# The last batch of an adapted layer and its routed update: two half batches made one whole one

## What is computed

```python
def _L0_cond_ref(x, adapter_mapping, W, b, lora_As, lora_Bs):
    base_out = jnp.einsum('bti,oi->bto', x, W) + b
    lora_h = jnp.einsum('bti,bir->btr', x, lora_As[adapter_mapping])
    lora_out = jnp.einsum('btr,bro->bto', lora_h, lora_Bs[adapter_mapping])
    return base_out + lora_out * SCALING

def _L0_ffn_ref(x, route_w, A, Bw):
    logits = jnp.einsum('bsd,ed->bse', x, route_w)
    topk_v, topk_idx = jax.lax.top_k(logits, 1)
    route_weight = jax.nn.one_hot(topk_idx[..., 0], E, dtype=logits.dtype) * topk_v
    h = jnp.einsum('bsd,erd->bser', x, A)
    out = jnp.einsum('bser,eor->bso', route_weight[..., None] * h, Bw) * SCALING
    return out

x = x + _L0_ffn_ref(_L0_cond_ref(x, ...), route_w, A, Bw)
```

## Time and profile before

| | us |
|---|---|
| median of 3 runs (lowest, highest) | 286.09 (285.75, 286.72) |
| the profiled execution | 285.52 |
| its span, first to last instruction | 283.7 |
| PE busy | 278.7 |
| VectorE busy | 201.8 |
| ACT busy | 112.5 |
| TensorE clock granted | 1.00 throughout |

### The profile page before, as it was taken

How to read it: one execution, slowest core, us unless ns; L and a number is a source line. 1 busy time by engine, 2 the same in 40 slices (tenths; PEclk the granted TensorE clock), 3 DMA queues, 4 the chain that set the end, 5 groups by cost and what they waited for, 6 DMA issues and landing times.

```text
span 283.7 us, 4398 instructions
## 1 busy us (share of the span) xinstructions
PE 278.7 (98%) x1699; PEld 225.3 (79%) x1699; DVE 201.8 (71%) x234; ACT 112.5 (40%) x166; POOL 15.0 (5%) x46
## 2 busy tenths in 40 slices
PE   8999999999999999999999999999999999999994
PEld 5999999997766885888588758857885887588994
DVE  0052200077598999699789969996998798699975
ACT  0001301196786532734274355427432742442300
POOL 7600030000000000000000000000000000000000
PEclk9999999999999999999999999999999999999999
DMA  7999999999991066849967993999399769636668
GB/s 241 404 407 395 399 413 412 373 398 417 418 419 70 39 259 234 358 151 405 400 231 258 425 386 136 373 393 395 137 379 409 267 211 398 281 148 249 267 237 285
DMA packets 19303, 88.52 MB, mean 312 GB/s; under 512 B 2378, under 2 KB 4818, under 8 KB 11474
## 3 DMA queue, kind: packets, MB, share of 16 engines
q1 hardware_dynamic: 16128, 85.15, 76.8%
q10 hardware_dynamic: 3154, 3.09, 3.3%
HBM read 54.60 MB, written 33.55 MB: 311 GB/s over the span
## 4 chain that ended last, share of the span: by engine, by line
PE 98%; DVE 0%; DVEq 0%; issue 0%
PE bank_out L693 16%; PE bank_h L770 11%; PE bank_h L771 10%; PE bank_h L772 10%; PE bank_out L730 10%; PE bank_out L732 10%; PE bank_out L731 10%; PE bank_e L755 10%; PE bank_e L693 1%; PE bank_l L706 1%; PE bank_l L693 1%; PE bank_h L693 1%; PE bank_r L693 1%; PE bank_h L699 1%; PE bank_r L790 1%; PE bank_h L783 1%
## 5 line engine op out<-in xcount | busy, mean ns | idle before, releaser
L433 ACT ACTIVATE x_hi<-x_ring 128x1024 fp32r<-128x1024 f32 (+1 forms) x72 | 68.9, 965 | 63.5 <-PE bank_h L772 63.0
L535 DVE TENSOR_TENSOR x_lo<-x_ring,x_hi 128x1024 fp32r<-128x1024 f32 (+1 forms) x72 | 78.8, 1103 | 9.3 <-ACT x_hi L433 8.7
L628 DVE TENSOR_TENSOR x_ring<-bank_out,x_ring 128x1024 f32<-128x1024 f32 (+1 forms) x71 | 78.5, 1107 | 1.7 <-PE bank_out L732 1.3
L770 PE MATMUL bank_h<-x_hi,m_hi 128*128 128x512 f32 (+1 forms) x144 | 53.5, 372 | 0.0
L771 PE MATMUL bank_h<-x_lo,m_hi 128*128 128x512 f32 (+1 forms) x144 | 52.7, 366 | 0.0
L772 PE MATMUL bank_h<-x_hi,m_lo 128*128 128x512 f32 (+1 forms) x144 | 52.6, 366 | 0.0
L730 PE MATMUL bank_out<-wh_hi,bw_hi 128*128 128x512 f32 (+1 forms) x143 | 52.5, 367 | 0.0
L731 PE MATMUL bank_out<-wh_lo,bw_hi 128*128 128x512 f32 (+1 forms) x143 | 52.4, 366 | 0.0
L732 PE MATMUL bank_out<-wh_hi,bw_lo 128*128 128x512 f32 (+1 forms) x143 | 52.4, 366 | 0.0
L770 PEld LDWEIGHTS bank_h<-x_hi,m_hi 128*128 128x128 f32 x144 | 27.1, 188 | 11.2 <-issue 5.9
L693 PE MATMUL bank_out<-pt,w_ring 128*128 128x136 f32 x288 | 34.5, 279 | 0.0
(11 more groups left out here) (96 smaller groups left out, 188.7 us busy)
## 6 DMA issues: line engine op xcount, KB each, us to landing
x_ring<-xT SPq DMA_DIRECT2D x32, 1024.0 KB, 7.8
outT<-x_ring SPq DMA_DIRECT2D x28, 1024.0 KB, 5.0
w_ring<-W SPq DMA_DIRECT2D x30, 512.0 KB, 10.8
outT<-x_ring SPq DMA_DIRECT2D x12, 256.0 KB, 2.7
x_ring<-loraB ACTq DMA_DIRECT2D x8, 128.0 KB, 10.2
la<-loraA ACTq DMA_DIRECT2D x8, 128.0 KB, 13.1
x_ring<-BwT SPq DMA_DIRECT2D x1, 1024.0 KB, 11.6
pt<-PT SPq DMA_DIRECT2D x3, 272.0 KB, 8.9
```

Source lines behind the costliest of these rows:

```text
L433: act.activation(out, in_, ACT.Copy).then_inc(done, 1)
L535: dve.tensor_tensor(out, a, b, ALU.subtract).then_inc(done, 1)
L628: dve.tensor_tensor(x, out_banks(u, j), x, ALU.add).then_inc(v_out, 1)
L770: mm(h, m_hi[:, c, :], hi, start=(c == 0), stop=False)
```

## The change

Batch 7 is one unit of 512 tokens, like the others. The four single banks are made two tensors of two banks, `bank_eh` and `bank_rl`, of which the old names are views. The output steps of batch 7 go in turn through `bank_eh`, `bank_out0`, `bank_out1`, `bank_rl`; three output steps of batch 6 are held. Batch 7's steps are stored by 512 KB each, its last one as two chunks of 256 KB. The order of x in memory is then the same for all batches.

```diff
-        bank_e = psum("bank_e", [P, T])
-        bank_h = psum("bank_h", [P, T])
-        bank_r = psum("bank_r", [P, T])
-        bank_l = psum("bank_l", [P, T])
+        bank_eh = psum("bank_eh", [P, 2, T])
+        bank_rl = psum("bank_rl", [P, 2, T])
+        bank_e, bank_h = bank_eh[:, 0, :], bank_eh[:, 1, :]
+        bank_r, bank_l = bank_rl[:, 0, :], bank_rl[:, 1, :]
...
-        UNITS = [(b, 0, T) for b in range(NB - 1)] + [(NB - 1, t, T // 2) for t in (0, T // 2)]
-        NU = len(UNITS)
-
-        HELD = [2] * (NU - 1) + [3]
+        HELD = [2] * (NB - 1) + [3]
...
+        def w_bank(blk):
+
+            return (*bank_out, bank_eh, bank_rl)[blk] if blk < OPEN else bank_out[blk % 2]
+
+        def out_bank(b, j):
+
+            if b < NB - 1:
+                return bank_out[j % 2]
+            return (bank_eh, *bank_out, bank_rl)[j % 4]
+
+        def store_last(eng, c0, c1):
+
+            j = c0 // 2
+            k = NPIECES - NQ + 2 * T * j // PIECE
+            at = T * c0 % PIECE
+            eng.wait_ge(v_out, NP2 * (NB - 1) + (j + 1 if c1 - c0 == 2 else c1 - j))
+            eng.dma_start(outT[k, :, at:at + (c1 - c0) * T], x_ring[:, k % XRING, at:at + (c1 - c0) * T]).then_inc(d_last, 16)
...
-            for u in range(NB - 1, NU):
-                for j in range(NP2):
-                    if u < NU - 1 or j % 2 == 0:
-                        store_pair(sp, u, j)
-            store_single(sp, 1)
+            for j in range(0, NP2 - 1, 2):
+                store_last(sp, 2 * j, 2 * j + 2)
+            store_last(sp, C - 1, C)
...
             for j in range(1, NP2 - 1, 2):
-                store_pair(act, NU - 1, j)
-            store_single(act, 0)
+                store_last(act, 2 * j, 2 * j + 2)
+            store_last(act, C - 2, C - 1)
...
-            def out_pair(u, j):
-                nt = UNITS[u][2]
-                if u == 0 and j < 2:
-                    pe.wait_ge(v_m, M_LOTS[-1])
+            def out_pair(b, j):
+                if b == 0 and j < 2:
+                    pe.wait_ge(v_m, NWB)
+                elif b < NB - 1:
+                    pe.wait_ge(v_out, NP2 * b + j - 1)
+                elif j == 0:
+                    pe.wait_ge(v_two, NB)
+                    pe.wait_ge(v_wh, NB)
+                elif j == 3:
+                    pe.wait_ge(v_w, NB)
+                    pe.wait_ge(v_ahead, NB)
                 else:
-                    pe.wait_ge(v_out, pairs_added(u, j))
+                    pe.wait_ge(v_out, NP2 * b + j - (2 if j < 3 else 3))
```

More of the change, by code:

```diff
@@ L215, in loads_in_slot, with x_pair @@
             return n // WRING + (1 if n % WRING else 0)
[L217 to L223, removed]
         def x_landed(eng, k):
             eng.wait_ge(d_x[k % XRING], 16 * (k // XRING + 1))
[L229 to L234, removed]
-            nt = UNITS[u][2]
[L237 to L251, removed]
+        def x_pair(b, j):
+            at = 2 * T * j % PIECE
+            return x_ring[:, (NQ * b + 2 * T * j // PIECE) % XRING, at:at + 2 * T].rearrange("p (c t) -> p c t", c=2)
         WARM_UP = 8
@@ L437, in m_block, with split_hi @@
                 act.wait_ge(t_w, DONE[n])
[L438 to L447, removed]
+                sums = w_bank(n)[:, :, 0:PN]
+                copy(m_hi[:, 2 * n:2 * n + 2, :], sums[:, :, E:PN], a_m)
+                for i in range(2):
+                    copy(ext[i][:, 2 * n:2 * n + 2, 0:E], sums[:, :, 0:E], a_m)
+            def split_hi(b, j):
+                g = NP2 * b + j
+                if b == 0 and j < SRING:
                     act.wait_ge(t_w, NWP - WRING + j + 1)
@@ L491, in _ @@
                 m_block(n)
[L493 to L499, removed]
+            for b in range(NB):
+                act.wait_ge(t_ext, b + 1)
+                if b >= 1:
+                    act.wait_ge(v_two, b)
+                act.activation(e_top[:, :], bank_e[2 * GROUP:4 * GROUP, :], ACT.Identity,
+                               bias=e_bias[:, 0:1]).then_inc(a_top, 1)
                 for j in range(NP2):
-                    if j < 2 and short(u):
-                        split_hi(u, SRING + j)
-                    if j == 0 and leads(u):
+                    if j == 0:
                         act.wait_ge(v_two, b + 1)
@@ L507, in _ @@
                         copy(e_odd[:, :], e_two[GROUP:2 * GROUP, :], a_odd)
[L508 removed]
+                    if j == EHI_AT:
                         act.wait_ge(v_sum, b + 1)
@@ L537, in m_block, with split_lo @@
             def m_block(n):
[L538 to L546, removed]
+                dve.wait_ge(a_m, 3 * (n + 1))
+                sub(m_lo[:, 2 * n:2 * n + 2, :], w_bank(n)[:, :, E:PN], m_hi[:, 2 * n:2 * n + 2, :], v_m)
+            def split_lo(b, j):
+                g = NP2 * b + j
+                if b == 0 and j < SRING:
                     dve.wait_ge(t_w, NWP - SRING + j + 1)
@@ L610, in weight, with weigh @@
                                          op0=ALU.is_ge, op1=ALU.mult).then_inc(v_w, 1)
-            def weigh(u):
-                b, t0, nt = UNITS[u]
-                dve.wait_ge(t_main, NP2 * (u + 1))
+            def weigh(b):
+                dve.wait_ge(t_main, NP2 * (b + 1))
                 dve.wait_ge(v_w, b + 1)
[L616 to L628, removed]
+                dve.tensor_tensor(wh[:, :], bank_h, wh[:, :], ALU.mult).then_inc(v_wh, 1)
+            def weigh_lo(b):
+                dve.wait_ge(a_wh, b + 1)
+                if b >= 2:
+                    dve.wait_ge(t_out, NP2 * (b - 1))
+                sub(wh_lo[b % 2][:, :], wh[:, :], wh_hi[b % 2][:, :], v_whlo)
@@ L630, in _, with add_x @@
+            def add_x(b, j):
+                x = x_pair(b, j)
+                dve.wait_ge(t_out, NP2 * b + j + 1)
+                dve.tensor_tensor(x, out_bank(b, j)[:, :, :], x, ALU.add).then_inc(v_out, 1)
             dve.wait_ge(g_const, CONSTS)
             split_lo(0, SRING - 1)
-            for u, (b, _, _) in enumerate(UNITS):
+            for b in range(NB):
                 for j in range(NP2):
-                    if j == 0 and leads(u):
+                    if j == 0:
                         sum_two(b)
-                    if j < 2 and short(u):
-                        split_lo(u, SRING + j)
-                    if j == 0 and leads(u):
@@ L648, in _ @@
                     if j < SRING:
-                        if j >= 2 or not short(u):
-                            split_lo(u, SRING + j)
-                    elif u + 1 < NU:
-                        split_lo(u + 1, j - SRING)
-                    if u >= 1 and 1 <= j <= NP2 - HELD[u]:
-                        add_x(u - 1, j - 1)
-                if u >= 1:
-                    weigh(u)
-                    add_x(u - 1, NP2 - HELD[u])
-                weigh_lo(u)
-                if u >= 1:
-                    for j in range(NP2 - HELD[u] + 1, NP2):
-                        add_x(u - 1, j)
+                        split_lo(b, SRING + j)
+                    elif b + 1 < NB:
+                        split_lo(b + 1, j - SRING)
@@ L662, in _ @@
+                    if b >= 1 and 1 <= j <= NP2 - HELD[b]:
+                        add_x(b - 1, j - 1)
+                if b >= 1:
+                    weigh(b)
+                    add_x(b - 1, NP2 - HELD[b])
+                weigh_lo(b)
+                if b >= 1:
+                    for j in range(NP2 - HELD[b] + 1, NP2):
+                        add_x(b - 1, j)
             for j in range(NP2 - 1):
-                add_x(NU - 1, j)
+                add_x(NB - 1, j)
             for i in range(2):
-                x = x_pair(NU - 1, NP2 - 1)[:, i, :]
@@ L789, in _ @@
                             pe.wait_ge(v_w, b)
[L790 to L793 removed]
+                        mm(bank_r, beats[:, :], ahead[:, :], start=True, stop=True).then_inc(t_count, 1)
+                if b >= 1:
+                    for j in range(NP2 - HELD[b], NP2):
+                        out_pair(b - 1, j)
             for j in range(NP2):
[L795 removed]
+                out_pair(NB - 1, j)
 def kernel(x, itok_B_0_23, L0_cond_W, L0_cond_b, L0_cond_lora_As, L0_cond_lora_Bs, L0_ffn_route_w, L0_ffn_A, L0_ffn_Bw):
```

171 lines of the change are left out of this document (60 added, 111 removed).

## The result

| | before | after |
|---|---|---|
| median of 7 runs each, us | 286.09 (285.49 to 286.77) | 287.46 (287.11 to 288.00) |
| profiled execution, us | 285.52 | 287.79 |
| its span, us | 283.7 | 286.0 |
| PE matmuls | 1699 | 1602 |
| DMA engines full until about | 282.0 | 283.3 |

The account below looks back on a forecast made before the run. The stores, about 0.9 us behind the adds, were taken to bound the end. PE -1.48, wait +0.15 and VectorE's tail +0.4 were overridden by the store queue: net +0.3 on 285.52, 285.8, plus 0.57 to the median: 286.4 us, range 285.3 to 287.6.

Parts of the forecast that it names:

- PE: Batch 7's matmuls at 512 columns instead of 256: last matmul ends 1.48 us earlier, before a new wait of 0.15.
- The wait before the third held step: Batch 6's third held step must wait for VectorE's add of the first: about 0.15 us of new PE wait.
- VectorE: Batch 7's adds keep up with PE; the last ends at 279.5, 0.9 us before today's 280.40.
- The rate of the stores: Seven 512 KB stores with 4 KB runs move at 399 GB/s, taken from loads of W, in 9.2 us.
- Rival B: Store queue from 269.5: 512 KB stores go no faster than today's tail, 356 GB/s; +1.4, 287.5 us; chance 0.22.
- The end that all this was held against: Old kernel's last store, read as through at 282.38; the changed kernel's end was forecast at 282.7.
- the sum of the queue: Last stores put through one queue from 269.5, engines never idle: 2.5 + 9.2 + 1.5, end 282.7, +0.3.
- What the prediction said it would be wrong by: Queue gaps after 270, last store landing within 2.8 us of issue, or PE gaining less than 1 us.
- about 4 us: Sign at the end: the last store lands about 4 us after its issue, against 2.8 before.
- The forecast's own case: Whole kernel: stores bound the end, net +0.3, 286.4 us; chance 0.58, mostly within 0.3% of before.
- 356 with 2 KB runs: Old kernel's store tail, 275 to 282: a full queue moving 356 GB/s, taken as the store rate's lower end.

Follow-up runs that it names:

- after_two_held: Changed kernel with 128 more PE instructions, batch 6's last two 1 MB stores as four of 512 KB, and two held steps instead of three: 285.90 us, 1.0000 of before.
- after_moved: Changed kernel with 128 more PE instructions (alternating waits on met semaphores), moving PE's last instruction packet from 275.0 to 259.6: 286.49 us, 1.0016 of before.
- before_twos: Kernel before with batch 7's stores two output steps at a time (512 KB, 4 KB runs), all but the last two steps: 286.39 us, 1.0019 of before.
- after_waits: Changed kernel with 96 waits added to PE's preparation, 57 left after compiling, instruction packet moved to 270.0: 287.17 us, 1.0058 of before.
- after_split: Changed kernel with batch 6's last two 1 MB stores made four of 512 KB, each behind its own add: 286.67 us, 1.0038 of before.
- after_split_waits: Changed kernel with batch 6's last two 1 MB stores as four of 512 KB and 96 waits added on PE: 286.72 us, 1.0033 of before.
- after_few_stores: Changed kernel without the stores of batch 7's output steps 0 to 5 (3 MB unwritten), all computing kept: 285.55 us, 0.9985 of before.
- before_moved: Kernel before with 128 more PE instructions, moving PE's instruction packet from 266.9 to 275.9: 287.30 us, 1.0047 of before.
- before_waits: Kernel before with 96 waits added to PE's preparation, instruction packet moved from 266.9 to 264.8: 285.93 us, 1.0008 of before.

## Why the prediction was right and wrong

PE: right. 1.48 less a wait of 0.15 was forecast, 1.32 measured.

The wait before the third held step: the mechanism was right (VectorE's first held add, late by a margin of under 0.1). That step's first matmul and the one after it each start 0.34 behind the one ahead (266.24, 266.58, 266.92), 0.23 late together against the forecast 0.15; after_two_held, without the wait, has the last matmul 0.12 earlier. The expected effect on the end was nothing, and it was nothing.

VectorE: adds were to end 0.9 earlier; they end 0.8 earlier from S.

The rate of the stores: 399 was taken, 398 and 401 were measured over ten microseconds. The stream was to start its last 5.24 MB at 269.5, S + 28.4; the store was issued at 269.53 and, with the 0.73 of the earlier trace rows, started at S + 28.6. It was to be through at 282.7, S + 41.6; after_moved, with nothing in its way, is through at S + 41.80. Rival B's mechanism, 4 KB stores at 356, is refuted, though its sum of 287.5 is the nearest to what was measured. The rate of 358 that the Trainium skill, "DMA: Bandwidth & Descriptors", section "Bandwidth", calls binding does not bind here either: 398 over ten microseconds disagrees with it.

The end that all this was held against was read too early: 282.38 takes the 0.38 of the slice from 282 to 283 for a full queue that stops, but the last data packet of before ends at 282.78, S + 41.71. By last data, after_moved is thus only 0.09 later than before; by the end of the span it is 0.41 later.

**The step that failed is the sum of the queue, "they never idle", +0.3.** It treats 16 engines as one pipe that is through for all of them at once. One of them had 1.10 us of another job in the stretch, which the other 15 could not take over, and the store is complete only when the slowest has finished. The sum lacked a term, an instruction packet of PE in the full stretch, worth +0.97 in medians (287.46 to 286.49; 0.94 by the two ratios to before). Without it the change costs 0.53 (286.49 against 285.96 for before beside it; 1.0016 times, 1.0005 to 1.0028), which is the +0.3 with an error of 0.2. What the prediction said it would be wrong by (a gap after 270, a last store landing within 2.8, PE's gain under 1) looked in the wrong places; the sign that did fail was the last store's "about 4 us", which was 5.3.

That 287.46 still lies in the stated range, 285.3 to 287.6, is luck. The upper end was rival B in full, a slow rate that the runs refute, and the missing term happened to be small enough to stay under it. The forecast's own case, with most of its chance within 0.3% of before, did not come: the change costs 0.49%.

A second reading was wrong without harm: "356 with 2 KB runs" as the rate that sets the tail. The engines are busier per byte there, but the rate is that of arrival (before_twos). That made rival B look likelier than it was, and hid that the old kernel's end hangs on its adds more than on its queue.

Open: what sets the length of the lone stretch. It is 1.7 us in after, 1.6 in after_waits, in after_split and in after_split_waits, behind packets of 1.10, 1.66, 1.11 and 0.96, so it doesn't follow the packet's own time. Moving the packet takes the lone engine away in the changed kernel, the loss comes with it in the old one, and on idle engines (after_few_stores) it does no harm. That shows the cause, but by position only: no run kept the packet in place and made it shorter.

## What to carry to other kernels

When a kernel ends on a full DMA stretch, look at the share of the last microsecond, and at gaps in the middle: 0.06 is one engine of 16 working alone, and the question is what held it up; the packets of PE's instruction queue ahead of it are the first suspect, and adding or removing PE instructions far away moves them. Set a gain on the computing engine against the bytes still to be stored behind its last result: here a 1.3 us shorter PE was given back by larger and later last stores. And where the producer delivers at the very rate that a stretch shows, faster transfers gain nothing.

## What the runs showed of the hardware

A 16 KB instruction packet of PE took, where it fell among the stores of the last batches, 0.96 to 1.66 us of one DMA engine (1.10 in after, 1.66 in after_waits, 0.96 in before and in after_split_waits). A sole engine moved 25 GB/s. Behind a packet that fell among stores one engine was left working alone: at the end in after (283.5 to 285.2), in the middle in before (269.0 to 269.5) and in before_moved (277.2 to 277.8), where SP's issue of a store took 1.17 us in place of 0.33 and 15 engines stood.

The start differs between executions of one code. In after's profiled execution the first 16 matmuls on `head_sb` were slower than in before's, with one source line in both:

```profile
L619 PE MATMUL bank_out<-head_sb x16: 279/434/434, 4.4 to 7.3; 128*128 128x136 f32 x16
```

```profile
L693 PE MATMUL bank_out<-head_sb x16: 279/279/383, 4.2 to 6.2; 128*128 128x136 f32 x16
```

(Least, median and greatest ns.) That is about the 0.62 by which S lies later. It doesn't belong to the change: after_waits has S at 241.03, before_waits at 241.79. Over the thirteen profiled executions S lies between 241.03 and 242.54. What sets it stays open: the granted clock is 1.00 from 4 to 8 us in both executions, so the rows don't show a lower clock behind the 434 ns.
